# A transformer block on one chip: softmax denominators through ScalarE, two banks for their sums and three for the scores

## What is computed

```python
# x: (8, 2048, 4096)
qkv = layernorm(x) @ w_in.T                 # 6144 columns: 32 q, 8 k, 8 v heads
q, k = rope(q), rope(k)
scores = q @ k.T / sqrt(128)                # causal mask, 4 query heads share one k/v head
probs = softmax(scores)
attn = (probs @ v) @ w_out.T
x = x + layernorm(attn)
y = ((xf * in_scale) @ sign(weight).T) * out_scale + bias    # scales from a softmax router
x = x + layernorm(y)
```

## Time and profile before

| | us |
|---|---|
| median of the runs (2 runs: 9631.35 and 9777.6) | 9704.48 |
| the profiled execution | 9630.94 |
| its span, slowest core (core 5) | 9629.4 |
| spans of the other cores | 9544.8 to 9597.8 |
| attention in that span, first score product to last multiplication | 2435 to 5861 |

### The profile page before, as it was taken

The page is one execution under the profiler, slowest core; times in us unless marked ns, Lnnn a source line. Parts: engine busy times, 40 slices in busy tenths (PEclk is TensorE's granted clock), DMA queues, the critical chain, the costliest instruction groups (busy, mean ns, idle before and its releaser), DMA issues.

```text
span 9629.4 us, 67201 instructions; the slowest of 8 cores (9544.8 to 9629.4 us)
## 1 busy us (share of the span) xinstructions
PE 6343.9 (66%) x22496; PEld 2166.4 (22%) x22496; DVE 1823.5 (19%) x1540; ACT 1752.4 (18%) x2929; POOL 248.2 (3%) x283
## 2 busy tenths in 40 slices
PE   1277777786567778888888886888901078888200
PEld 1133333332111111111111112333400023333000
DVE  3211111111231121111111110000044440000233
ACT  2200000001332332222222220000022211111111
POOL 0011111100000000000000000000000000000000
PEclk6688888898555555555555556999955579999555
DMA  2221112221100000000000003222122212211343
GB/s 89 72 40 38 36 39 40 40 49 61 43 18 15 6 17 11 5 5 5 4 4 4 4 4 99 51 51 51 32 109 109 109 52 50 50 35 45 104 128 120
DMA packets 118321, 442.99 MB, mean 46 GB/s; under 512 B 13665, under 2 KB 87521, under 8 KB 88033
## 3 DMA queue, kind: packets, MB, share of 16 engines
q0 software_dynamic: 16912, 119.74, 6.8%
q10 hardware_dynamic: 12962, 176.18, 5.2%
q1 hardware_dynamic: 88128, 142.78, 4.2%
HBM read 415.78 MB, written 142.61 MB: 58 GB/s over the span
## 4 chain that ended last, share of the span: by engine, by line
PE 65%; DMA 13%; DVE 12%; ACT 5%; issue 3%; another core or an unknown queue 1%; POOL 1%; ACTq 0%; DVEq 0%; POOLq 0%; SPq 0%
PE PA L543 6%; PE PB L358 5%; PE PA L358 5%; DVE recT_sb L604 4%; DMA wq_sb<-wqkv 4%; PE PB L561 3%; PE PB L571 3%; PE PE L536 3%; PE PF L536 3%; PE PB L852 3%; PE PA L852 3%; PE PB L690 3%; PE PA L690 3%; DMA x_t<-xin 3%; DMA x_t<-x2s 3%
## 5 line engine op out<-in xcount | busy, mean ns | idle before, releaser
L604 DVE RECIPROCAL recT_sb<-PA 1x512 f32<-1x512 f32 x128 | 428.2, 3346 | 2110.1 <-PE PA L543 2110.1
L543 PE MATMUL PA<-ptb,ones_bf 128*1 128x512 bf16 (+3 forms) x1280 | 665.6, 520 | 0.0
L607 PE MATMUL PA<-recT_sb,ones_f 1*128 1x512 f32 x256 | 261.2, 1121 | 460.5 <-DVE recT_sb L604 460.5
L358 PE MATMUL PB<-arena,wq_sb 128*128 128x512 bf16 x2048 | 471.8, 393 | 127.8 <-DMA wq_sb<-wqkv 127.8
L358 PE MATMUL PA<-arena,wq_sb 128*128 128x512 bf16 x2048 | 470.0, 392 | 110.2 <-DMA wq_sb<-wqkv 110.2
L593 ACT ACTIVATE ptb<-PB 128x512 bf16<-128x512 f32 (+1 forms) x640 | 333.6, 573 | 625.8 <-PE PB L571 614.6
L561 PE MATMUL PB<-q_sb,k_sb 128*128 128x512 bf16 (+1 forms) x640 | 371.7, 581 | 1.1
L571 PE MATMUL PB<-nmxT_sb,ones_bf 1*128 1x512 bf16 (+1 forms) x640 | 371.8, 581 | 0.0
L852 PE MATMUL PB<-wslot,arena 128*128 128x512 bf16 x1344 | 302.9, 384 | 69.0 <-ACT wslot L822 69.0
L536 PE MATMUL PF<-ptb,vtm 128*128 128x512 bf16 (+3 forms) x640 | 347.2, 542 | 0.0
L536 PE MATMUL PE<-ptb,vtm 128*128 128x512 bf16 (+3 forms) x640 | 347.1, 542 | 0.0
(11 more groups left out here) (192 smaller groups left out, 6398.4 us busy)
## 6 DMA issues: line engine op xcount, KB each, us to landing
x_t<-xin ACTq DMA_DIRECT2D x32, 2048.0 KB, 9.3
wq_sb<-wqkv POOLq DMA_DIRECT2D x48, 1024.0 KB, 9.4
wslot<-wout POOLq DMA_DIRECT2D x32, 1024.0 KB, 17.2
x2s<-ln2tmp SPq DMA_DIRECT2D x16, 2048.0 KB, 6.2
wslot<-wffn POOLq DMA_DIRECT2D x32, 1024.0 KB, 15.6
x_t<-x2s ACTq DMA_DIRECT2D x16, 2048.0 KB
out<-y_t SPq DMA_DIRECT2D x16, 2048.0 KB, 12.2
Qs<-qout_sb SPq DMA_DIRECT2D x128, 128.0 KB, 7.5
```

The lines of the kernel that those rows point to most:

```text
L358: do("tensor", lambda e, p=p, ec=ec, tb=tb, a=sl["ap"]: e.matmul(a[:, :], wq_sb[p][:, ec * 128:(ec + 1) * 128], arena[:, ec * S + tb * 512 ...
L543: e.matmul(sums_ap[0:1, j0 * 128: j0 * 128 + cw], ones_bf1[:, 0:1], ptb[pb][:, j0 * 128: j0 * 128 + cw], start=(kc == 0), stop=(kc == nkc ...
L604: vrc = do("vector", lambda e, sp=sp: e.reciprocal(recT_sb[sp][0:1, :], sums_ap[0:1, 0:512]), inc="sV", waits=(("sT", pe_grp),))
L607: do("tensor", lambda e, sp=sp: e.matmul(sums_ap[:, 0:512], ones_f[:, :], recT_sb[sp][0:1, :], start=True, stop=True), inc="sT", waits=((" ...
```

## The change

The reciprocal of the sums moves from VectorE to ScalarE, as exp(−ln(sum)) in three instructions. The row of sums no longer lies in one bank for all groups, but in PD for even and in the upper half of PA for odd ones. PD is thereby no longer one of the banks for the scores, of which three are left, and every index into them is kc % 3 in place of kc % 4. The value that the first value product of a group waits for (`bc_last`) is kept for each of the two sums banks.

```diff
     stbank = [dict(ap=PB[:, 0:512], exp=0), dict(ap=PB[:, 512:1024], exp=0),
-              dict(ap=PC[:, :], exp=0), dict(ap=PD[:, :], exp=0)]
-    sums_ap = PA[:, 512:1024]
+              dict(ap=PC[:, :], exp=0)]
+    sums_banks = [PD[:, :], PA[:, 512:1024]]
...
-    bc_last = [0]
+    bc_last = [0, 0]
...
+        sums_ap = sums_banks[g % 2]
         pend_pv = []
 
         def emit_pv(kc, pb, j0, cw):
-            wpv = (("sA", stbank[kc % 4]["exp"]),)
+            wpv = (("sA", stbank[kc % 3]["exp"]),)
             if kc == 0:
-                wpv = wpv + (("sV", pvb["free"]), ("sA", bc_last[0]))
+                wpv = wpv + (("sV", pvb["free"]), ("sA", bc_last[g % 2]))
...
-            bk = stbank[kc % 4]
+            bk = stbank[kc % 3]
...
-                bk = stbank[kci % 4]
+                bk = stbank[kci % 3]
...
-        vrc = do("vector", lambda e, sp=sp: e.reciprocal(
-            recT_sb[sp][0:1, :], sums_ap[0:1, 0:512]), inc="sV",
-            waits=(("sT", pe_grp),))
+        a1 = do("scalar", lambda e, sp=sp: e.activation(
+            recT_sb[sp][0:1, :], sums_ap[0:1, 0:512], AF.Ln, bias=0.0, scale=1.0),
+            inc="sA", waits=(("sT", pe_grp),))
+        a2 = do("scalar", lambda e, sp=sp: e.mul(
+            recT_sb[sp][0:1, :], recT_sb[sp][0:1, :], -1.0), inc="sA",
+            waits=(("sA", a1),))
+        a3 = do("scalar", lambda e, sp=sp: e.activation(
+            recT_sb[sp][0:1, :], recT_sb[sp][0:1, :], AF.Exp, bias=0.0, scale=1.0),
+            inc="sA", waits=(("sA", a2),))
         do("tensor", lambda e, sp=sp: e.matmul(
             sums_ap[:, 0:512], ones_f[:, :], recT_sb[sp][0:1, :],
-            start=True, stop=True), inc="sT", waits=(("sV", vrc),))
+            start=True, stop=True), inc="sT", waits=(("sA", a3),))
...
-        bc_last[0] = bc
+        bc_last[g % 2] = bc
```

## The result

The changed kernel takes 10,123.54 us (median of 11 runs) against 9634.12 us (10 runs of the kernel before, beside it), a ratio of 1.0486 with a 95% interval of 1.0446 to 1.0526: slower by 4.9%. The forecast was 10,126 us.

What follows compares the result with a forecast made beforehand. TensorE was taken to bound attention, by its own work and its standstills. Stalls of 665 us less 170 us saved give +495 us on 9630.94, so 10,126 us, range 10,035 to 10,255.

Steps and rivals of the forecast that it cites:

- What bounds attention: Attention: TensorE sets the pace by its own work, 2787 of 3426 us, and its standstills, at clock 0.50.
- The reciprocal on ScalarE: Group end: TensorE's wait for the denominators falls from 3.60 to 2.27 us, 128 times, saving 170 us (159 to 175).
- Second sums bank and VectorE's relief: Group end: neither the second bank for the sums nor the 3.35 us taken off VectorE is worth anything.
- Score product 3 of block 0: With three score banks it waits for exponential 0: 0.19 us late in block 0, hidden in blocks 1 to 3.
- The value products: Even chunks' value products wait for the exponential three chunks on: 512 stalls, 665 us together, 77 us either way.
- at the first pair ... 1.45, the same: First pair of value products in a group: stall of 1.45 us, the same as for other full pairs.
- The full pairs: Value products of full pairs of chunks: each stalls 1.44 us, until the second exponential has ended.
- The weight loads: Stalled value products: weights are not loaded during the wait; if they were, the sum would be about 50 us less.
- lift the clock: Rival, attention: shorter pauses raise TensorE's clock from 0.50, bringing the total near 9110 us; chance 4%.
- slack to hide the stall: Rival, value products: unseen slack hides the wait, leaving only the gain, 9461 us, −1.8%; chance 3%.
- The sum: Whole kernel: 665 − 170 = +495 us on 9630.94 us, giving 10,126 us, 5.1% slower; chance 91%.

Runs made afterwards that it cites:

- the exact wait: The changed kernel, but each value product waits for the exponential of its own chunk, its number carried along with the chunk; 9400.32 us (median of 4).
- the denominators alone: The kernel before with the reciprocal replaced by logarithm, sign and exponential on ScalarE; four score banks, one sums bank; 9392.07 us (median of 4).
- the other order: The changed kernel with the three waits of a group's first value product reordered: output bank, copy, exponential last; 10,203 us (2 executions).
- the last experiment: The kernel of e5_defer, but with the reciprocal on VectorE as in the kernel before; 9059.06 us (5 runs), ratio 0.9385.
- e5_defer: Changed kernel, each value product waiting for its own chunk's exponential, group's end moved behind the next group's first four score products; 9020.78 us, ratio 0.9266.

## Why the prediction was right

**What bounds attention.** TensorE in program order, as read; the clock stayed at 0.50 in every part of it, before and after.

**The reciprocal on ScalarE, −170 us.** Measured −168.9 us alone, with 2.27 us a group, the sum of the rows to the hundredth. The new exponential took 0.63 us, the value that was chosen between 0.59 and 0.72. No row of ScalarE is a table load: the three instructions have 0.08 to 0.10 us between them, as L506, L509 and L511 had.

**Second sums bank and VectorE's relief, nothing.** Right: the exact wait and the denominators alone differ by 6.4 us, in the other direction. What the bank is worth only the moved group end shows.

**Score product 3 of block 0, 0.19 us late.** Right: 6.4 us over 32 groups, 0.20 each, and hidden in the other blocks.

**The value products, +665 us.** The mechanism was shown by taking the wait away (−681.5) and by adding it and nothing else (+682.1). The size was 23 us low (682.1, and 6.4 for block 0's score product, against 665). The step that fell short is "at the first pair ... 1.45, the same": the first value product of a group has three waits, and the two behind the late one cost 0.21 us more. Over 128 groups that is 27 us, and the other order gave back 27.6. All other stalls together came out 5 us lower than forecast: 653.9 us (3903.8 − 3249.9) against 659, which is 665 without the 0.19 us of block 0. The full pairs at 1.46 us by starts, against 1.44, were right.

**The weight loads.** At the stalled value product the load starts at 4716.37, 0.03 us ahead of the matmul and after the wait, as at L501 before; in all 512 stalls it is 0.02 to 0.04 us. None of these loads passed the wait that stands before it. The row decided, and rightly. The Trainium skill (TensorE: Matmul & The Clock Gate, Part 2) says that loads are pulled ahead of matmuls in flight; it says nothing there of a wait ahead of the load, and to read the rule as holding across one was the forecast's own step, which these stalls do not bear out. The 50 us named for it were too high as well: 0.03 us in 512 stalls are 15 us.

**The rivals.** Shorter pauses did not lift the clock, neither with stalls nor in the two experiments without them that kept the pause of 2.27 us. There was no slack to hide the stall.

**The sum.** +495 us forecast; +519 us in the stretch, +489.4 between the medians of whole times (10,123.54 − 9634.12), and +468 by the ratio of 1.0486. The terms were 24 us low together, 23 in the stalls and 1 in the denominators. That the median hit 10,126 within 3 us is luck: the other stages differ by more than that from run to run, and here they made up for the 24 us that attention took beyond the forecast.

## What to carry to other kernels

A table that holds the last event of each buffer is read too late when the consumer is written out after a newer producer has entered its own; with one buffer fewer, the same lookup names another event. It still guards the data and only waits longer, and the order of instructions looks the same. So carry the event with the work item. A second bank for a result frees nothing until the instruction that waits is placed behind other work, and once it is, a slow operation on an idle engine costs as little as a fast one: with the group's end moved the stretch is 709 us shorter than before with the slow reciprocal (3412.4 − 2703.9) and 689 with the fast one, some of it from the risen clock, while the faster reciprocal alone gave 169.

## What the runs showed of the hardware that was not expected

The order of the waits on one instruction has a price. With the wait that ends last written first, the two others cost 0.21 us together after it, though they had long been met (1.59 against 1.38 us of idle time in most groups; half of it for each is an estimate from that); with the late one written last, they cost nothing.

In the two kernels whose group ends do not stop TensorE, the granted clock of attention leaves its lower level of 1.2 GHz now and then. In the six others it was 0.50 in every 20 us of the stretch, on all 8 cores. Core 1 of the last experiment, in the columns of the earlier trace rows, and as the last row core 4 of `e5_defer`:

```profile
3740.00:3760.00 20.00, 20.00 (x46) 4.35 (x45) 3.35 (x1) 5.86 (x13) 0.00 (x0) 0.50 0.00 0
3760.00:3780.00 20.00, 19.02 (x58) 5.11 (x57) 5.14 (x4) 9.88 (x20) 0.00 (x0) 0.84 0.02 8
4100.00:5100.00 1000.00, 999.90 (x2080) 200.30 (x2079) 129.33 (x88) 319.28 (x611) 0.00 (x0) 0.50 0.01 4
...
4100.00:5100.00 1000.00, 1000.00 (x2079) 200.33 (x2077) 33.22 (x60) 376.12 (x704) 0.00 (x0) 0.50 0.01 4
```

For some tens of microseconds at a time it is up (58 matmuls in 20 us in place of 46), and in block 3, where TensorE works for 1000 us with next to no gap, it stays at 0.50. The places differ from core to core. So steady work did not suffice to lift it here, against what the Trainium skill (TensorE: Matmul & The Clock Gate, Part 1) leads one to expect. Why it rises where it does, and not in block 3, stays open.
